# Routed experts: gathers ahead of older scatters, and the down projection as three fp32r products with its splits shared out

## The reference

```python
xn = _layernorm(x)
def expert_body(acc, ws):
    gw, uw, dw, cwe = ws
    y = silu(xn @ gw.T) * (xn @ uw.T) @ dw.T
    return (acc + cwe[:, None] * y, None)
routed = scan(expert_body, 0, (gate_w, up_w, down_w, cw.T))
x = x + attention(xn) + routed + shared_mlp(xn)
```

## Time and profile before

| | us |
|---|---|
| runs | 1150.83, 1152.27, 1143.80 |
| median | 1150.83 |
| profiled execution | 1154.67 |
| its span | 1152.0 |
| TensorE busy | 1051.4 (91%) |
| VectorE busy | 788.4 (68%) |
| ScalarE busy | 638.0 (55%) |
| GpSimd busy | 506.3 (44%) |
| granted TensorE clock, mean | 0.963 |

### The profile page before, as it was taken

How to read it: one execution, slowest core, us unless ns; L and a number is a source line. 1 busy time by engine, 2 the same in 40 slices (tenths; PEclk the granted TensorE clock), 3 DMA queues, 4 the chain that set the end, 5 groups by cost and what they waited for, 6 DMA issues and landing times. The chain is left out here.

```text
span 1152.0 us, 19013 instructions
## 1 busy us (share of the span) xinstructions
PE 1051.4 (91%) x5379; PEld 818.1 (71%) x5380; DVE 788.4 (68%) x1713; ACT 638.0 (55%) x1275; POOL 506.3 (44%) x566
## 2 busy tenths in 40 slices
PE   5999947988899999999999999979879999999994
PEld 4857835766687777777878778758767777777773
DVE  6732413666688868888888888655567777778772
ACT  3322211355677868788777777851245555555551
POOL 0003802588755655566566565540013433333331
PEclk9999978898999989999999999989989999999998
DMA  6988995276344354634445545038595334443332
GB/s 210 330 341 318 118 293 195 62 117 123 72 139 127 68 158 121 160 102 126 125 127 148 147 117 151 1 126 291 198 360 121 66 65 73 73 72 64 67 72 36
DMA packets 105768, 163.60 MB, mean 142 GB/s; under 512 B 53936, under 2 KB 64432, under 8 KB 102096
## 3 DMA queue, kind: packets, MB, share of 16 engines
q1 hardware_dynamic: 95344, 141.82, 43.2%
q0 software_dynamic: 9760, 20.49, 9.9%
q10 hardware_dynamic: 576, 0.26, 0.1%
HBM read 101.25 MB, written 61.28 MB: 141 GB/s over the span
## 5 line engine op out<-in xcount | busy, mean ns | idle before, releaser
L1186 POOL TENSOR_TENSOR prob_lo<-prob,prob_hi 128x512 fp32r<-128x512 f32 (+2 forms) x320 | 308.4, 978 | 201.9 <-ACT prob_hi L1231 140.7
L1224 ACT ACTIVATE prob<-ps_s 128x512 f32<-128x512 f32 (+3 forms) x384 | 188.4, 491 | 124.9 <-PE ps_s L1451 70.2
L1231 ACT ACTIVATE prob_hi<-prob 128x512 fp32r<-128x512 f32 (+3 forms) x384 | 198.5, 517 | 12.7 <-ACT row_stage L1205 11.9
L1864 DVE TENSOR_TENSOR rw_lo<-gu_sb,rw_hi 128x704 fp32r<-128x704 f32 x156 | 139.0, 893 | 48.9 <-ACT rw_hi L1799 44.7
L1778 POOL DMA_INDIRECT out<-work,rows x39 | 61.6, 1580 | 244.4 <-DVE rows L1825 119.2
L1294 DVE CUSTOM_DVE_ANT_0 ps_m<-ps_m,causal 128x384 f32<-128x384 f32 (+3 forms) x256 | 126.7, 496 | 60.6 <-PE ps_m L1422 56.7
L1799 ACT ACTIVATE rw_hi<-gu_sb 128x704 fp32r x156 | 123.5, 793 | 48.0 <-PE ps_ru L1897 32.1
L1422 PE MATMUL ps_m<-ks,qs 96*128 96x512 f32 (+3 forms) x384 | 141.7, 370 | 8.3 <-DVE vs L1400 7.3
L1446 PE MATMUL ps_s<-qs,ks 97*128 97x512 f32 (+3 forms) x384 | 138.9, 362 | 9.2 <-ACT prob L1224 8.3
L1469 PE MATMUL ps_o<-prob_hi,vs 128*66 128x512 f32 (+3 forms) x384 | 131.7, 343 | 8.7 <-issue 6.0
L1471 PE MATMUL ps_o<-prob_lo,vs 128*66 128x512 f32 (+3 forms) x384 | 130.8, 341 | 0.0
(11 more groups left out here) (203 smaller groups left out, 2349.2 us busy)
## 6 DMA issues: line engine op xcount, KB each, us to landing
xt<-xt_blocks SPq DMA_DIRECT2D x7, 2048.0 KB
v_rows<-work SPq DMA_DIRECT2D x16, 512.0 KB, 3.1
xt_blocks<-xt SPq DMA_DIRECT2D x4, 2048.0 KB, 11.2
qk_hi<-work SPq DMA_DIRECT2D x8, 1024.0 KB, 4.1
qk_lo<-work SPq DMA_DIRECT2D x8, 1024.0 KB, 7.1
qs<-qk_hi SPq DMA_DIRECT2D x64, 128.0 KB, 2.9
ks<-qk_hi SPq DMA_DIRECT2D x64, 128.0 KB, 3.2
vs<-v_rows SPq DMA_DIRECT2D x32, 256.0 KB, 4.3
```

Source lines behind the costliest of these rows:

```text
L1186: nc.gpsimd.tensor_tensor(prob_lo[:, s % NPL, 0:w], prob[:, s % NP, 0:w], prob_hi[:, s % NPH, 0:w].bitcast(F32), ALU.subtract).then_inc(lo ...
L1224: nc.scalar.activation(prob[:, s % NP, 0:w], ps_s[s % NS][:, 0:w], ACT.Exp, scale=SCALE).then_inc(exp_done, 1)
L1231: nc.scalar.activation(prob_hi[:, s % NPH, 0:w], prob[:, s % NP, 0:w], ACT.Copy).then_inc(hi_ready, 1)
L1864: nc.vector.tensor_tensor(w_lo[:, k, :], chunk(e, k), w_hi[:, k, :].bitcast(F32), ALU.subtract).then_inc(w_lo_ready, 1)
```

## The change

- Row numbers are read from `slot_table` by the DMAs themselves; `rows` and VectorE's copies into it are gone.
- GpSimd's list is written out without a loop: gather j, then two subtractions for tile j-4, then scatter j-5.
- The down projection becomes nine fp32r products a tile: `rd_hi` and `rd_lo` hold the split down weights, `hid_t_hi` and `hid_t_lo` the split hidden units, one buffer each. ScalarE makes `rd_hi` (three chunks) and `hid_t_hi` (two reads of `ps_ht`), GpSimd the first two chunks of `rd_lo`, VectorE the third and `hid_t_lo`. So ScalarE, GpSimd and VectorE each load the expert number for it, and TensorE no longer does.
- `rd_lo` lies where `y_tile` was, so ScalarE waits for all its stores before its first routed operation.
- On TensorE the order in a step is turn_x, turn_h instead of turn_h, turn_x.

```diff
+def row_numbers(slot_table, j):
+    return bass.IndirectOffsetOnAxis(slot_table[:, j, 0:1].bitcast(I32), 0)
...
-                pool.wait_ge(rows_ready, GS)
                 for j in range(GS):
                     pool.wait_ge(tile_ready, j + 1)
                     pool.sem_inc(passed, 1)
                     nc.gpsimd.indirect_dma_start(
                         attended[:, j, :], None, xn_dram,
-                        bass.IndirectOffsetOnAxis(rows[:, j:j + 1], 0)).then_inc(gathered[j], 16)
+                        row_numbers(slot_table, j)).then_inc(gathered[j], 16)
...
-        units = work[:, 3 * R:4 * R, :].rearrange("p a d -> p (a d)")
-        silu, hid = [units[:, n * HR * F:(n + 1) * HR * F].rearrange("p (u f) -> p u f", u=HR)
+        free = work_at + 2 * R * D * 4
+        hid_t_hi, hid_t_lo = [
+            nc.alloc_sbuf_tensor_at(f"hid_t{n}", [P, NF, P], F32R, offset=free + n * NF * P * 4)
+            for n in range(2)]
+        free += 2 * NF * P * 4
+        d_hi = nc.alloc_sbuf_tensor_at("rd_hi", [P, NF, D], F32R, offset=free)
+        d_lo = nc.alloc_sbuf_tensor_at("rd_lo", [P, NF, D], F32R, offset=y_at)
+        free += NF * D * 4
+        silu, hid = [nc.alloc_sbuf_tensor_at(f"units{n}", [P, HR, F], F32, offset=free + n * HR * F * 4)
                      for n in range(2)]
-        hid_t = work[:, 2 * R:2 * R + HR, 0:NF * P].rearrange("p u (k t) -> p u k t", k=NF)
+        assert free + 2 * HR * F * 4 <= work_at + NT * D * 4
...
-                def gather(i, c):
-                    j = U * i + c
-                    if isinstance(j, int) and j < GS:
-                        return
-                    wait(pool, x_turned, j - R + 1)
-                    wait(pool, rows_ready, j + 1)
+                def gather(j):
+                    pool.wait_ge(x_turned, j - R + 1)
                     pool.sem_inc(passed, 1)
                     nc.gpsimd.indirect_dma_start(
-                        xg[:, c % R, :], None, xn_dram,
-                        bass.IndirectOffsetOnAxis(rows[:, c:c + 1], 0)).then_inc(gathered[c % R], 16)
-                def scatter(i, c):
-                    j = U * i + c
-                    if isinstance(j, int) and j == 0:
+                        xg[:, j % R, :], None, xn_dram,
+                        row_numbers(slot_table, j)).then_inc(gathered[j % R], 16)
+                def scatter(j):
+                    if j == 0:
                         for n in range(YS):
                             pool.wait_ge(y_stored[n], 16 * (NT // YS))
                     wait(pool, scattered, 16 * j)
-                    wait(pool, y_ready, j + 1)
+                    pool.wait_ge(y_ready, j + 1)
                     pool.sem_inc(passed, 1)
                     nc.gpsimd.indirect_dma_start(
-                        out, bass.IndirectOffsetOnAxis(rows[:, c:c + 1], 0), y[:, c % R, :], None,
+                        out, row_numbers(slot_table, j), y[:, j % R, :], None,
                         compute_op=ALU.add).then_inc(scattered, 16)
-                pipeline(pool, NST, U, [(0, gather), (3, scatter)])
+                def down_lo(j):
+                    e = expert(pool, j)
+                    for k in range(NF - 1):
+                        pool.wait_ge(d_hi_ready, NF * j + k + 1)
+                        nc.gpsimd.tensor_tensor(d_lo[:, k, :], down_chunk(e, k),
+                                                d_hi[:, k, :].bitcast(F32),
+                                                ALU.subtract).then_inc(d_lo_ready, 1)
+                for j in range(GS, NST + 5):
+                    if j < NST:
+                        gather(j)
+                    if 0 <= j - 4 < NST:
+                        down_lo(j - 4)
+                    if 0 <= j - 5 < NST:
+                        scatter(j - 5)
                 pool.wait_ge(scattered, 16 * NST)
...
+                def turn_h(i, c):
+                    j = U * i + c
+                    w = FCH[-1][1]
+                    wait(act, h_turned, j + 1)
+                    wait(act, y_done, j)
+                    nc.scalar.activation(hid_t_hi[:, 0:2, :], ps_h[:, 0:2, :],
+                                         ACT.Copy).then_inc(h_hi_ready, 1)
+                    nc.scalar.activation(hid_t_hi[0:w, 2, :], ps_h[0:w, 2, :],
+                                         ACT.Copy).then_inc(h_hi_ready, 1)
+                def down_hi(i, c):
+                    j = U * i + c
+                    e = expert(act, j)
+                    act.wait_ge(experts_ready, e + 1)
+                    for k, (f0, w) in enumerate(FCH):
+                        if k < NF - 1:
+                            wait(act, d_used, (NF - 1) * (j - 1) + k + 1)
+                        else:
+                            wait(act, y_done, j)
+                        nc.scalar.activation(d_hi[0:w, k, :], down_chunk(e, k),
+                                             ACT.Copy).then_inc(d_hi_ready, 1)
+                for n in range(YS):
+                    act.wait_ge(y_stored[n], 16 * (NT // YS))
+                pipeline(act, NST, U, [(2, turn_h), (2, down_hi), (0, turn_x), (0, first_chunks),
+                                       (1, gate_unit), (0, last_chunk)], back=R)
...
                 def turn_h(i, c):
                     j = U * i + c
-                    wait(dve, h_turned, j + 1)
-                    wait(dve, y_done, j - HR + 1)
-                    nc.vector.tensor_copy(hid_t[:, c % HR, 0:2, :], ps_h[:, 0:2, :]).then_inc(h_ready, 1)
                     w = FCH[-1][1]
-                    nc.vector.tensor_copy(hid_t[0:w, c % HR, 2, :], ps_h[0:w, 2, :]).then_inc(h_ready, 1)
+                    wait(dve, h_hi_ready, 2 * (j + 1))
+                    for rows_of, ks in ((P, slice(0, 2)), (w, slice(2, 3))):
+                        nc.vector.tensor_tensor(hid_t_lo[0:rows_of, ks, :], ps_h[0:rows_of, ks, :],
+                                                hid_t_hi[0:rows_of, ks, :].bitcast(F32),
+                                                ALU.subtract).then_inc(h_lo_ready, 1)
+                def last_down_lo(i, c):
+                    j = U * i + c
+                    e = expert(dve, j)
+                    w = FCH[-1][1]
+                    wait(dve, d_hi_ready, NF * (j + 1))
+                    nc.vector.tensor_tensor(d_lo[0:w, NF - 1, :], down_chunk(e, NF - 1),
+                                            d_hi[0:w, NF - 1, :].bitcast(F32),
+                                            ALU.subtract).then_inc(d_last_ready, 1)
...
-                pipeline(dve, NST, U, [(0, row_numbers), (4, turn_h), (2, x_lo), (2, first_chunks),
-                                       (3, hidden), (2, last_chunk), (4, weigh)], back=U)
+                pipeline(dve, NST, U, [(4, turn_h), (4, last_down_lo), (2, x_lo),
+                                       (2, first_chunks), (3, hidden), (2, last_chunk),
+                                       (4, weigh)], back=U)
...
                 def turn_h(i, c):
                     j = U * i + c
                     wait(pe, hid_ready, j + 1)
-                    wait(pe, h_ready, 2 * j)
+                    wait(pe, h_lo_ready, 2 * j)
                     for k, (f0, w) in enumerate(FCH):
                         last = nc.tensor.transpose(ps_h[0:w, k, :], hid[:, c % HR, f0:f0 + w], ident[:, :])
                     last.then_inc(h_turned, 1)
                 def down(i, c):
                     j = U * i + c
-                    e = expert(pe, j)
-                    pe.wait_ge(experts_ready, e + 1)
-                    wait(pe, h_ready, 2 * (j + 1))
+                    wait(pe, h_lo_ready, 2 * (j + 1))
                     wait(pe, y_ready, j - 1)
                     for k, (f0, w) in enumerate(FCH):
-                        last = nc.tensor.matmul(
-                            ps_y[c % 2][:, :], hid_t[0:w, c % HR, k, :],
-                            d_sb[0:w, bass.ds(e * NF + k, 1), :].rearrange("p a d -> p (a d)"),
-                            start=(k == 0), stop=(k == NF - 1))
-                    last.then_inc(y_done, 1)
-                pipeline(pe, NST, U, [(2, turn_h), (0, turn_x), (1, gate_up), (2, down)], back=R)
+                        if k < NF - 1:
+                            wait(pe, d_lo_ready, (NF - 1) * j + k + 1)
+                        else:
+                            wait(pe, d_last_ready, j + 1)
+                        for a, b in ((hid_t_hi, d_hi), (hid_t_hi, d_lo), (hid_t_lo, d_hi)):
+                            last = nc.tensor.matmul(ps_y[c % 2][:, :], a[0:w, k, :], b[0:w, k, :],
+                                                    start=(k == 0 and a is hid_t_hi and b is d_hi),
+                                                    stop=(k == NF - 1 and a is hid_t_lo))
+                        if k == NF - 1:
+                            last.then_inc(y_done, 1)
+                        else:
+                            last.then_inc(d_used, 1)
```

(33 more changed lines are left out.)

12 lines of the change are left out of this document (6 added, 6 removed).

## The result

The changed kernel takes 1173.46 us (1172.58 to 1175.82, 4 runs) against 1150.83 for the kernel before (3 runs); a fourth run of the kernel before, of 3586.91 us, is left out. The ratio of the two sets of runs is 1.0216, with a 95% interval of 1.0162 to 1.027, so the change makes the kernel 2% slower, some 25 us. The profiled execution has a span of 1170.9 us, 18.9 more than before.

The account below looks back on a forecast made before the run. It took TensorE to bound the kernel before, then a once-a-tile loop plus collision at 8.56 us: 32.0 for 33 tiles, 2.3 for the first six, 4.4 for the ends, +38.7, giving 1189 us, range 1158 to 1226.

Parts of the forecast that it names:

- the rival without a collision: Routed stage: GpSimd's and VectorE's subtractions do not block each other, 7.91 us a tile, +13.4, 1164 us; chance 0.17.
- the collision: Routed tiles: GpSimd's rd_lo subtractions and VectorE's rd_lo and rw_lo block each other in SBUF, 0.65 more, 8.56 us a tile.
- loop of 7.91 us: Once a tile: ps_ht reads, rd_hi, xg_hi, rw_hi, rw_lo, hidden product, transposes, next ps_ht reads; 7.91 us without collision.
- Both terms: TensorE, routed tiles: gather stops of 12.0 us gone, nine down products save 0.50 a tile; 6.70 us a tile, 31.5 less.
- the number load of 0.38 before rw_hi: ScalarE, routed tile: loading the expert's number after xg_hi stops it for 0.38 us before the first rw_hi.
- The rival "faster": Routed stage: ScalarE's number loads run ahead hidden, 7.21 us a tile, TensorE stays the bound, -13.9, 1137 us; chance 0.08.
- 7.57: Routed stage: the tile length in us at which the change's summed effect is nothing, 4.4 for the ends included.
- The rival "GpSimd twice ahead": Routed tiles: both GpSimd subtractions run before VectorE's rd_lo, 9.1 to 9.5 us a tile, 1211 to 1226 us; chance 0.23.
- The first six tiles: Start of the routed stage: six tiles at 8.56 us instead of 8.17, +2.3 us.
- 3 was forecast: End of the routed stage: the last scatter stands behind GpSimd's two subtractions of tile 38, 3 us more.
- the 1.4 at the start: Start of the routed stage: ScalarE waits for all y_tile stores, 2.3 us late at most, 1.4 taken.
- That rival: Routed stage: TensorE, idle 1.9 of 8.6 us, drops to 1.2 GHz and its 6.70 would pass 11; chance 0.05.

Follow-up runs that it names:

- Experiment 1: Changed kernel without GpSimd's two rd_lo subtractions, rd_hi standing in for rd_lo in the middle product of chunks 0 and 1: 1143.51 us, 0.9962 to the kernel before.
- experiment 3: Kernel before with GpSimd's order alone changed, gather j then scatter j-5: 1128.05 us, 0.9836; with row numbers from slot_table too: 1127.52 us, 0.9841.
- experiment 7: Changed kernel with rd_hi ahead of the ps_ht reads on ScalarE and no rd_lo on GpSimd, rd_hi standing in: 1122.07 us, 0.9797 to the kernel before.
- experiment 4: Changed kernel with each gather put behind the scatter of the tile four back, as before the change: 1267.06 us, 1.1025 to the kernel before.
- experiment 5: Changed kernel with one swap in ScalarE's list, the three rd_hi ahead of the two ps_ht reads: 1155.57 us, 1.0054 to the kernel before.
- experiment 6: Changed kernel with all three rd_lo on VectorE: with rd_hi first 1150.20 us, 1.0 to the kernel before; in its own order 1150.76 us, 1.0019.

## Why the prediction was right, and where its sizes were off

The forecast was 1189 us, in a range of 1158 to 1226; 1173.46 was measured. By the number alone the rival without a collision, 1164, was nearer. Experiment 1 decides against it: the collision is there, and the rival's number came near only because its loop of 7.91 us was itself 0.4 too long. So the causes and the direction were right, and the size was some 14 us too large: +38.7 for the stage's +24.0 and the ratio's +25.

- **What is removed.** Both terms held: no stop for a gather, 7.20 us a tile alone [experiment 3]; nine products 0.23 apart, 6.68 in the best tiles against 6.70 [experiment 7].
- **The loop.** Right in its order and in its place, the wait before the ps_ht transposes. Its length alone was 7.91 forecast, 7.5 measured [experiment 1]. The term that was too long is the number load of 0.38 before rw_hi: there is none, rw_hi starts at 1005.14, before xg_hi's end at 1005.23. Only the load behind the short ps_ht reads showed, 0.46 where I had 0.32 (0.3 in experiment 1). The earlier trace rows show the loads behind ScalarE that has just been idle or short of work. The rival "faster" rested on this very point; half of it came true, and 7.57 was the point at which it decides: with the loop at 7.5 and no collision the kernel is 0.4% faster than before.
- **The collision.** Forecast 0.65 us a tile, in this order: VectorE's rd_lo waits for GpSimd's first, GpSimd's second holds up rw_lo. Measured 0.82 - 0.69 = 0.13 on rd_lo and 2.98 - 2.50 = 0.48 on rw_lo, of which 0.54 reach the tile; with the 0.19 of ScalarE's longer number load, which I had not foreseen, a tile is 0.73 longer than without. The two rd_lo take 3.00 us together: the first 1.30, where I had used 1.32, and the second 1.74, since it waits for VectorE's.
- **The rival "GpSimd twice ahead"** happened in 2 of the 39 tiles of this kernel (rd_lo of 2.19 and 2.20 us at 862.8 and 871.7), and it is real: in experiments 4 and 5 VectorE stands still through both in 31 and 19 of 39 tiles. That it gets in after the first is not a rule; I had made it one from a single row.
- **The sum.** Of +38.7 the 33 steady tiles were to give 32.0; 32 of them gave 24.0, mostly for the number load of 0.38. The first six tiles were to give +2.3 and gave -6.7: I priced them at the new tile length against 8.17, though these six held 4.3 us of gather stops, the longest among them, which I had myself removed. The granted clock was also lower there before, 0.76 in 832 to 850; what that was worth is not separated. From the turning of tile 38 to the end it is 6.7 more: 2.7 until its ps_ht transposes and 4.0 behind them, where 3 was forecast. Of the 1.4 at the start 0.5 is seen: ScalarE's first xg_hi starts 1.15 after the x transposes, 0.67 before. Of the -5.1 at the start, 3.8 is attention's variation from one execution to another.

The granted clock did not fall in the changed kernel's steady tiles, with TensorE busy 43.62 of 50 us (87%, where about 80% was forecast). That rival is real too: in experiment 4, with 77.89 busy of 100, it was 0.86.

## What to carry to other kernels

Before work is moved to an idle engine, walk the list of each engine once round a tile and look for a chain that comes back to its start: it can bound the kernel though no engine is full, and swapping two neighbours in one list can open it (7.50 to 6.85 us a tile here). Look also at which instructions of other engines slow down beside the moved ones: with GpSimd's two subtractions on VectorE instead, the kernel was 23 us faster. And when a change has two halves, run them apart: here one is worth 1.6% and the other hid it.

## What was not expected of the hardware

- VectorE's two-input operation can stand still through two GpSimd subtractions in a row, 2.1 us for one of 0.87 (experiment 5), or get in between them as in 37 of the 39 tiles of the changed kernel. What decides was not settled. The Trainium skill ("SBUF — State Buffer", on the two separate sides of SBUF) has whoever starts first hold the SBUF ports that VectorE and GpSimd share for the whole instruction; that agrees with those 37 tiles, not with this row. Nor does it agree with experiment 4, where the rw_lo of 1064.90 starts 0.64 us before GpSimd's first subtraction and still lasts 3.91 us, through both.
- A turn of ScalarE's loop took 2.4 us before its next instruction (experiment 5; 2.63 of idle ScalarE in experiment 6). In the changed kernel, where ScalarE idles 2.0 us a tile, the tiles at the turns are at most 0.1 longer than the others; without that slack the two turns cost 3.6 and 3.0 us, and some 6 us were won by writing the list out.
- The load of an expert number cost ScalarE 0.3 to 0.5 us behind the short ps_ht reads (0.46 at 1003.08) and nothing behind a queue of operations (no gap before rw_hi at 1005.14).
